# Splitting the softmax probabilities into halves on ACT and DVE instead of on ACT, DVE and POOL

## What is computed

```python
scale, shift = jnp.split(emb @ W_emb + b_emb, 2, axis=-1)
xn = _rms_norm(x, g_norm) * (1.0 + scale) + shift
q, k, v = (xn @ W_qkv) by heads;  q, k = _rms_norm(q, g_q), _rms_norm(k, g_k)
attn = softmax(q @ k^T * d ** (-0.5))
o = attn @ v
x = x + (o + o @ W_out)
x = x + (causal_conv(x, taps=cond) + b)
```

## Time and profile before

| | |
|---|---|
| median of 3 runs | 2824.38 us |
| lowest, highest | 2818.74, 2824.69 us |
| the profiled execution: its own time | 2817.93 us |
| the profiled execution: span | 2815.9 us |
| mean granted TensorE clock | 0.938 |
| busy PE / DVE / ACT / POOL | 2441.3 / 2036.0 / 1588.2 / 1743.5 us |

### The profile page before, as it was taken

The page is one execution under the profiler, slowest core; times in us unless marked ns, Lnnn a source line. Parts: engine busy times, 40 slices in busy tenths (PEclk is TensorE's granted clock), DMA queues, the critical chain, the costliest instruction groups (busy, mean ns, idle before and its releaser), DMA issues. The chain is left out here.

```text
span 2815.9 us, 57892 instructions
## 1 busy us (share of the span) xinstructions
PE 2441.3 (87%) x20690; PEld 1557.1 (55%) x20690; DVE 2036.0 (72%) x3096; ACT 1588.2 (56%) x2575; POOL 1743.5 (62%) x972
## 2 busy tenths in 40 slices
PE   2467888888889999999999898999999999999788
PEld 0034445454446666666666565666666565666477
DVE  7656666655667788788788787788877677777655
ACT  2246555555556666566666566566665555556511
POOL 0057766666777777666667676677666676666510
PEclk8689899888899999999999999999999999999899
DMA  6858777777988888889998888889987878778751
GB/s 258 349 133 168 151 157 151 146 162 158 198 182 173 174 187 169 171 181 209 196 200 175 174 171 173 172 164 223 186 173 151 164 149 154 149 146 158 144 163 61
DMA packets 1234893, 487.27 MB, mean 173 GB/s; under 512 B 1139520, under 2 KB 1196992, under 8 KB 1232064
## 3 DMA queue, kind: packets, MB, share of 16 engines
q1 hardware_dynamic: 1234624, 483.63, 81.2%
HBM read 141.13 MB, written 57.18 MB: 70 GB/s over the span
## 5 line engine op out<-in xcount | busy, mean ns | idle before, releaser
L1132 POOL TENSOR_TENSOR p_pair<-prob,p_pair 128x1024 f16<-128x1024 f32 x512 | 1144.9, 2250 | 670.9 <-ACT p_pair L919 580.5
L800 PE MATMUL proj<-w_sb,xn_sb 128*128 128x384 f16 x6144 | 1029.0, 327 | 30.4 <-DMA xn_sb<-p_pair 28.9
L1217 DVE TENSOR_REDUCE neg<-scores 128x1 f32<-128x1024 f32 x512 | 623.4, 1218 | 397.3 <-PE scores L749 395.3
L911 ACT ACTIVATE prob<-scores,bias,l_scale 128x1024 f32<-128x1024 f32 x512 | 615.3, 1202 | 482.1 <-DVE bias L1220 452.2
L800 PEld LDWEIGHTS proj<-w_sb,xn_sb 128*128 128x128 f16 x6144 | 588.9, 98 | 430.2 <-DMA xn_sb<-p_pair 25.7
L749 PE MATMUL scores<-stack 64*128 64x512 f16 x3072 | 419.9, 411 | 133.9 <-ACT prob L911 110.2
L768 PE MATMUL values<-pT,v_pair 128*64 128x256 f16 x6144 | 412.0, 287 | 48.6 <-ACT inv_row L975 43.2
L768 PEld LDWEIGHTS values<-pT,v_pair 128*64 128x64 f16 x6144 | 335.0, 115 | 141.4 <-issue 108.1
L749 PEld LDWEIGHTS scores<-stack 64*128 64x128 f16 x3072 | 137.8, 99 | 336.1 <-ACT prob L911 116.4
L824 PE MATMUL proj<-oT_in,wo 128*128 128x256 f16 x2304 | 269.2, 274 | 1.2
L919 ACT ACTIVATE p_pair<-prob 128x1024 f16<-128x1024 f32 x256 | 266.7, 1042 | 0.0
(11 more groups left out here) (127 smaller groups left out, 2180.9 us busy)
## 6 DMA issues: line engine op xcount, KB each, us to landing
w_sb<-w_dram SPq DMA_DIRECT2D x128, 384.0 KB, 4.0
o_dram<-oT_pair SPq DMA_DIRECT2D x128, 128.0 KB, 2.5
out<-acc SPq DMA_DIRECT2D x64, 256.0 KB, 2.7
wq_raw<-in_L_cond_W_qkv SPq DMA_DIRECT2D x8, 1536.0 KB, 10.4
w_dram<-wq_pair SPq DMA_DIRECT2D x8, 1536.0 KB, 7.5
x_in<-in_x SPq DMA_DIRECT2D x24, 512.0 KB, 4.3
oT_in<-o_dram SPq DMA_DIRECT2D x12, 1024.0 KB, 5.8
xr<-in_x SPq DMA_DIRECT2D x24, 512.0 KB, 3.8
```

The lines of the kernel that those rows point to most:

```text
L800: last = nc.tensor.matmul(proj[:, t % 2, 0:6 * DH], xn_sb[:, t, i * K + c, :], w_sb[:, c, j, :], start=(c == 0 and i == j == 0), stop=(c = ...
L911: nc.scalar.activation(prob[:, h, :], scores[:, h, :], ACT.Exp, bias=bias[:, s:s + 1], scale=const["l_scale"][:, 0:1], accum_out=total[:, ...
L1132: nc.gpsimd.tensor_tensor(p_pair[:, s % 4, 1, :], prob[:, h, :], p_pair[:, s % 4, 0, :], ALU.subtract).then_inc(lo_done, 1)
L1217: nc.vector.tensor_reduce(neg[:, s:s + 1], scores[:, h, :], axis=AX.X, op=ALU.max, negate=True).then_inc(max_done, 1)
```

## The change

The low halves of both heads go from POOL to DVE, the high half of head 1 goes from DVE to ACT, and one semaphore `hi_done` takes the place of two. `high_halves(w, 1)` goes behind the exponentials of period 6, `read_stacks` of misc ahead of the high halves of period 7. The second stacks go behind the output product of period 7 on PE. On POOL `half_low(w, 0)` moves from period 5 to 4 and `low_values(w, 1)` from 7 to 5. The output transposes of the first half, their reading, their store and one convolution go one period later.

```diff
--- before.py
+++ after.py
@@ -449,8 +449,7 @@
         max_done = sem("max_done")
         bias_done = sem("bias_done")
         exp_done = sem("exp_done")
-        hi_a = sem("hi_a")
-        hi_b = sem("hi_b")
+        hi_done = sem("hi_done")
         lo_done = sem("lo_done")
         pT_in = [sem(f"pT_in{i}") for i in range(8)]
         pv_done = sem("pv_done")
@@ -652,8 +651,6 @@
                         if outs:
                             load_xr(T, par)
                     if p == 2:
-                        if fins:
-                            store_out(T - 1, 1 - par, 0)
                         if xs and direct:
                             transpose_x(v, pair, xn_sb[:, K - 1], xn_in[K - 1])
                         elif xs:
@@ -662,6 +659,8 @@
                                 passed()
                             transpose_x(v, pair, pairT[:], xT_in)
                     if p == 3:
+                        if fins:
+                            store_out(T - 1, 1 - par, 0)
                         if begun:
                             store_o(u - 1, 3)
                         if xs and direct:
@@ -851,9 +850,6 @@
                         inverses(u, (p - 3) // 2)
                     elif p == 1 and begun:
                         inverses(u - 1, 3)
-                    if qkv and p == 7:
-                        stacks(w, 1, 1, misc[:], (h_ev, 4 * w + 2))
-                        stacks(w, 1, 0, proj[:, 0, :], (y_ev, 2 * T + 1) if outs else (qkv_ev, K * w + 7))
                     if qkv:
                         for t, q0, q1 in quarters[p]:
                             project(w, t, q0, q1, T - 1 if fins else None)
@@ -869,7 +865,10 @@
                     if qkv and p == 5:
                         stacks(w, 0, 0, misc[:], (f_ev, 2 * T if fins else 0))
                         stacks(w, 0, 1, proj[:, 1, :], (qkv_ev, K * w + 8))
-                    if fins and p == 0:
+                    if qkv and p == 7:
+                        stacks(w, 1, 1, misc[:], (h_ev, 4 * w + 2))
+                        stacks(w, 1, 0, proj[:, 0, :], (y_ev, 2 * T + 1) if outs else (qkv_ev, K * w + 7))
+                    if fins and p == 1:
                         out_transposes(T - 1, 0, (h_ev, 4 * u + 4))
                     if fins and p == 4:
                         out_transposes(T - 1, 1, (f_ev, 2 * T - 1))
@@ -912,11 +911,11 @@
                                      scale=const["l_scale"][:, 0:1],
                                      accum_out=total[:, par * NS + s:par * NS + s + 1]).then_inc(exp_done, 1)
 
-            def high(u, p):
-                s = 2 * p
+            def high(u, p, h):
+                s = 2 * p + h
                 act.wait_ge(exp_done, slot(u, s) + 1)
                 need(act, pT_in[(s + 4) % 8], 16 * (2 * u + (s + 4) // 8))
-                nc.scalar.activation(p_pair[:, s % 4, 0, :], prob[:, 0, :], ACT.Copy).then_inc(hi_a, 1)
+                nc.scalar.activation(p_pair[:, s % 4, 0, :], prob[:, h, :], ACT.Copy).then_inc(hi_done, 1)
 
             def read_projection(w, t):
                 hf = t // KH
@@ -1037,7 +1036,6 @@
                         if qkv:
                             read_stacks(w, 1 - par, 0, 0, 0, misc[:])
                             read_stacks(w, 1 - par, 0, 1, 1, proj[:, 1, :])
-                            high_halves(w, 1)
                     if p == 7:
                         o_high(u, 1)
                     exponent(u, p, 0, par)
@@ -1046,9 +1044,13 @@
                         inverse_rows(u, (p - 3) // 2)
                     elif p == 1 and begun:
                         inverse_rows(u - 1, 3)
-                    high(u, p)
-                    if p == 7 and qkv:
+                    if qkv and p == 6:
+                        high_halves(w, 1)
+                    if qkv and p == 7:
                         read_stacks(w, 1 - par, 1, 1, 2, misc[:])
+                    high(u, p, 0)
+                    high(u, p, 1)
+                    if qkv and p == 7:
                         read_stacks(w, 1 - par, 1, 0, 3, proj[:, 0, :])
                     if p == 0:
                         if qkv:
@@ -1056,11 +1058,11 @@
                         if begun:
                             read_inverses(u - 1, 2)
                     if p == 1:
-                        if fins:
-                            read_out(T - 1, 0)
                         if xs:
                             x_high(v, x_in[:], pair, (xT_in, 16 * u))
                     if p == 2:
+                        if fins:
+                            read_out(T - 1, 0)
                         if begun:
                             read_inverses(u - 1, 3)
                         if qkv:
@@ -1126,12 +1128,6 @@
 
         @block.gpsimd
         def _(pool):
-            def low(u, p, h):
-                s = 2 * p + h
-                pool.wait_ge((hi_a, hi_b)[h], K * u + p + 1)
-                nc.gpsimd.tensor_tensor(p_pair[:, s % 4, 1, :], prob[:, h, :], p_pair[:, s % 4, 0, :],
-                                        ALU.subtract).then_inc(lo_done, 1)
-
             def half_power(w, hf):
                 pool.wait_ge(h_ms, 2 * w + hf + 1)
                 need(pool, h_n, 2 * (2 * w + hf))
@@ -1181,19 +1177,16 @@
                     if p == 4 and qkv:
                         half_power(w, 0)
                         low_values(w, 1 - par, 0)
+                        half_low(w, 0)
                     if p == 5:
                         o_lower(u, 0)
                         if qkv:
-                            half_low(w, 0)
                             half_power(w, 1)
+                            low_values(w, 1 - par, 1)
                     if p == 6 and qkv:
                         half_low(w, 1)
                     if p == 7:
                         o_lower(u, 1)
-                    low(u, p, 0)
-                    low(u, p, 1)
-                    if p == 7 and qkv:
-                        low_values(w, 1 - par, 1)
 
             for v in range(K + 2):
                 if v >= 2:
@@ -1220,11 +1213,11 @@
                 nc.vector.tensor_scalar(bias[:, s:s + 1], neg[:, s:s + 1], const["l_scale"][:, 0:1], P_SHIFT,
                                         ALU.mult, ALU.add).then_inc(bias_done, 1)
 
-            def high(u, p):
-                s = 2 * p + 1
-                dve.wait_ge(exp_done, slot(u, s) + 1)
-                need(dve, pT_in[(s + 4) % 8], 16 * (2 * u + (s + 4) // 8))
-                nc.vector.tensor_copy(p_pair[:, s % 4, 0, :], prob[:, 1, :]).then_inc(hi_b, 1)
+            def low(u, p, h):
+                s = 2 * p + h
+                dve.wait_ge(hi_done, slot(u, s) + 1)
+                nc.vector.tensor_tensor(p_pair[:, s % 4, 1, :], prob[:, h, :], p_pair[:, s % 4, 0, :],
+                                        ALU.subtract).then_inc(lo_done, 1)
 
             def sums(w, hf):
                 n = 2 * w + hf
@@ -1323,10 +1316,11 @@
                             x_mean(v, par, 2)
                         if begun:
                             invert(u - 1, 3, 1 - par)
+                    if p == 1:
+                        if xs:
+                            x_shift(v, x_in[:])
                         if fins:
                             convolve(T - 1, 1 - par, 0, 1)
-                    if p == 1 and xs:
-                        x_shift(v, x_in[:])
                     if p in (2, 4, 6):
                         invert(u, p // 2 - 1, par)
                     if p == 2:
@@ -1342,7 +1336,8 @@
                         sums(w, 1)
                     if p == 7 and outs:
                         convolve(T, par, 0, 0)
-                    high(u, p)
+                    low(u, p, 0)
+                    low(u, p, 1)
                     if p == 0:
                         if begun:
                             scale_values(u - 1, 2)
```

## The result

The changed kernel takes 2856.36 us (median of 4 runs, 2854.15 to 2858.01) where the kernel before, measured beside it, takes 2823.36 us. The ratio is 1.0119, with a 95% interval of 1.0102 to 1.0137: slower by 1.2%. The forecast was 2851 us. The profiled execution took 2857.12 us, its span is 2855.0 us, and the mean granted clock is 0.931 instead of 0.938.

A forecast was written before the change was run, and what follows sets the result against it. The kernel was taken as PE-bound with gaps. Units 8 to 30 at 0.06 + 1.5 us gave +36, the first eight +1, the last −4: together +33 on 2817.9, 2851 us, range 2788 to 2888, chance 0.46.

The forecast's parts named there:

- The low half on DVE: DVE's 16 added low halves a unit, taken at 1.21 us each, 2.4 us a period.
- Periods 0 to 5 hide the longer chain: DVE is free 7.6 to 7.9 us after the row maximum; these periods last 9.0 to 10.8 us on PE: no cost.
- Rival 3: DVE becomes the bound, some 3 us a unit: +90, 2940 us; chance 0.05.
- M6 falls to S6's end: Period 5 to 6: row maximum M6 comes 3.3 us earlier; the 2.80 us wait before score product S7 goes.
- M6 to M7 grows and gives it back: Period 6 to 7: high_halves on ACT and half_low on POOL delay DVE's lows; the 3.3 us won are lost.
- The wait stands before the attend: Period 7: PE waits 3.4 to 4.7 us in one piece before the value product (attend), 4.88 us behind M7.
- The clock: Half-clock products behind the attend's wait: extra of 0 to 2.9 us a unit, taken as 1.5.
- S5 to S6: Interval between score products of periods 5 and 6, left as it was; S6 ends 10.7 us after row maximum M5.
- First eight units +1, last unit −4: First eight units: attend 27.8 us behind S5 against 27.65, +1 with clock; last unit: shorter chain and last lows, −4.
- The stacks and their read: no cost: Period 7: second stacks behind the output product on PE, read_stacks of misc ahead of ACT's high halves; no cost.
- Rival 1: half_low does not delay the lows, M7 less than 9 us behind M6: −30, 2788 us; chance 0.32.
- Rival 2: POOL's power blocks period 5's lows on DVE, M6 1.2 to 1.7 us later: +37 on the forecast, 2888; chance 0.08.

The follow-up runs named there:

- e9: e4 with read_out of period 5 and the second stacks' first read of period 7 ahead of the high halves, `inverses` of period 7 behind the second stacks; 2721.39 us.
- e8: Changed kernel with high_halves(w, 1) again ahead of period 6's exponentials, second stacks ahead of the output product, their reads behind the high halves; 2782.13 us.
- e7: Changed kernel with only high_halves(w, 1) put back on ACT ahead of the exponentials of period 6; 2763.93 us.
- e5: Changed kernel with high_halves(w, 1) of period 6 moved behind ACT's two high halves; 2760.03 us.
- e4: Kernel before with the new softmax split alone, both high halves on ACT, both low halves on DVE, old order kept; 2770.29 us.

## Why the prediction was right, and where not

The time was right (2851, measured 2856) and so was the sign: 33 us were added to the time before, and the medians differ by 33.0. But one part of the reasoning had the wrong place, and several terms cancelled.

- *The low half on DVE.* Taken at 1.21 us from the nearest row; the median of 512 is 1.219. Right.
- *Periods 0 to 5 hide the longer chain.* Right: S2 to S5 did not change at all, and DVE is busy 62.08 us in a unit of 78.47, not near 70 as I wrote: more of the old waiting for POOL came back than I had counted. Rival 3 is out.
- *M6 falls to S6's end.* Right: 1838.99 us, and S6 is through at 1838.96. The wait before S7 is gone in units 8 to 30. normalise's first multiply met low_values, 2.18 us instead of 1.21, as bounded.
- *M6 to M7 grows and gives it back.* Right in mechanism and nearly in size: 9.89 us, forecast 10.3, with the same two parts, high_halves on ACT and half_low against the lows. The forecast had both POOL instructions in the way; one was.
- *The wait stands before the attend.* This step failed. I followed DVE from the lows over scale_values to M7 and never asked who waits for scale_values itself. PE's `inverses` does, and it is queued ahead of the output product. So PE stood still where I had it at work on the output product, and did that product after the wait instead of ahead of one. M7 itself came where forecast, 22.78 us behind S5 (22.65), but the attend did not follow it by 4.88 us: it came 6.11 us later, when PE was through with its products.
- *The clock.* 1.5 us a unit was taken, on the attend and the product behind it; it fell on the output product, 1.58 us in the unit shown. Place wrong, size right. In this unit it is more than the 1.40 us by which the attend comes later than in the earlier trace rows. But the S7 of the earlier trace rows was itself slow, 2.74 us, and that is so in only 14 of the 23 units; I had built the sum on one of them. Over units 8 to 30 PE's busy time grew from 1683.8 to 1695.2 us and its idle time from 105.5 to 129.9: of the 35.8 us, 24.4 are more waiting and 11.4 slower products. My 36 had waits of 4.7 us for 3.3, and slow products of 1.5 us in place of the 1.27 by which S7 had been slow, so about 1.4 and 0.2 us a unit where 1.06 and 0.50 were measured. That the sums agree so closely is partly luck.
- *S5 to S6.* I left it as it was, and it grew by 0.64 us a unit (inside the 1.40): with two high halves ahead of it, read_out comes late and the first stacks wait 1.06 us. With read_out ahead of them (e9) S5-S6 is 10.17 us.
- *First eight units +1, last unit −4.* Units 1 to 7 gave −7.7. The stacks' wait fell to 1.52 us as forecast (1.4), but both contentions had been taken at their worst: M5 to M6 took 10.52 us (forecast 11.0), M6 to M7 9.88 (10.3), and the attend came 26.67 us behind S5 in most of these units, where 27.8 was forecast and 27.65 stood. The last unit gave +5.2: without projection PE meets the waits for scale_values (9.4 us before `inverses` in it, 5.6 before the change) and for the moved convolution (4.74 us, 3.90 before). The two errors cancel: the forecast had −3 for these units together, they gave −2.3 (with +0.2 in unit 0).
- *The stacks and their read: no cost.* They cost nothing, and e8 against e7 shows a gain that I had not seen: 18 us for moving both, most of it from the read ahead of the high halves.
- *Rival 1* (M7 early, a gain) did not come here. e5 and e7 come to a state like it by another way, with high_halves too out of the chain: M6 to M7 is 7.8 us (rival 1 had 9.0) and the time 2760 and 2764 us. *Rival 2*: DVE's lows of period 5 took 2.36 us for two, from 1833.02, while the power ran on POOL from 1832.01 to 1834.91. The Trainium skill (SBUF — State Buffer, "SBUF: two separate sides") would have them blocked until it ends; the measurement decides, and for this instruction they are not. All 62 lows that start while a power runs take 1.22 or 1.23 us. For half_low and low_values the trace agrees with the page: beside them the lows took 3.43 us instead of 2.36, and the first multiply 2.18 instead of 1.21.

The larger error lies outside the number. I priced the change as one thing. Split by experiment, it is a gain of 1.7% from the new split and a loss of more than that from one moved step, whose reason, the late end of normalise, the split itself takes away.

## What to carry to other kernels

When work is taken off one engine, work out again which waits are left before moving other steps around them: the step moved to dodge a wait may then stand in the new critical chain. For every instruction that gets later, list all who wait for it, on every engine, and what is queued behind each of those waits. Put steps that nobody needs soon behind the ones that end a chain, and a POOL and a DVE instruction that slow each other, as half_low and the lows did here (3.25 and 3.43 us instead of 2.26 and 2.36), where they don't overlap.

## What the runs showed of the hardware that was not expected

The length of a wait alone does not tell whether PE's clock falls behind it. In the changed kernel the wait of 3.92 us ahead of the output product of period 7 was followed by a product of over 3.5 us in all 23 units (4.37 us in the rows above). A wait of 1.82 us in the same place was followed by one in none of 23 units in e7 and e5, where the output product comes right behind `inverses`, but in 7 of 23 in e4 and in 4 of 23 in e8, where the second stacks stand between. Why is not shown. The 2.80 us before S7 in the kernel before were followed by a slow S7 in 14 of 23 units. POOL's power over 16 elements a partition, 2.90 us long, did not delay two DVE instructions of 128x1024 with two SBUF inputs, while a POOL subtraction of 128x512 did by about its own length of 1.1 us.
